# Attention moved 21 turns sooner in a graph layer paced by gathers, with TensorE's last stages written out by hand

## What is computed

```
msg   = relu(x[src] + edge_attr @ w_e + b_e)         # a gathered row of x for each edge
agg   = segment_sum(msg, dst)
local = bn(relu((x + agg) @ w1 + b1) @ w2 + b2 + x)
attn  = bn(attention within graphs of 32 nodes, 4 heads (x) @ out_w.T + out_b + x)
out   = local + attn
out   = bn(out + relu(out @ m_w1 + m_b1) @ m_w2 + m_b2)
y     = layernorm(x + out)
```

## Time and profile before

| | |
|---|---|
| device time, median of 3 runs | 1297.24 us (1296.20 to 1297.25) |
| profiled execution | 1296.03 us |
| its span, first to last instruction | 1294.2 us |
| TensorE busy | 1154.5 us (89%) |
| POOL busy | 944.9 us (73%) |
| VectorE / ScalarE busy | 826.7 us (64%) / 541.2 us (42%) |
| mean granted TensorE clock | 0.969 |

### The profile page before, as it was taken

One profiled execution on the slowest core, in us unless ns is written; L12 is line 12 of the kernel. 1 busy time (PEld: TensorE's weight loads), 2 busy tenths in 40 slices (PEclk: granted clock), 3 DMA queues, 4 the chain that ended last, 5 costly groups with the idle time before them and its releaser, 6 DMA issues.

```text
span 1294.2 us, 28246 instructions
## 1 busy us (share of the span) xinstructions
PE 1154.5 (89%) x7309; PEld 647.4 (50%) x7309; DVE 826.7 (64%) x2090; ACT 541.2 (42%) x1077; POOL 944.9 (73%) x1004
## 2 busy tenths in 40 slices
PE   6787989998899899998989999998989998998896
PEld 3444454544445444444544545454444555765675
DVE  5847486767566576755758666575756667557563
ACT  1343434444344435434344443443434443443353
POOL 7777777777777777777777777777777777675770
PEclk7898999999999999999999999999999998999999
DMA  8554555655555555565555555555655565554550
GB/s 316 154 170 141 175 156 175 174 173 180 170 165 169 164 182 172 160 183 148 183 173 175 165 165 176 166 175 174 172 164 154 183 183 147 168 160 126 175 155 26
DMA packets 119282, 216.50 MB, mean 167 GB/s; under 512 B 24784, under 2 KB 69584, under 8 KB 119120
## 3 DMA queue, kind: packets, MB, share of 16 engines
q0 software_dynamic: 47808, 130.61, 35.0%
q1 hardware_dynamic: 67312, 79.47, 19.6%
q10 hardware_dynamic: 4000, 4.61, 1.0%
HBM read 197.82 MB, written 16.78 MB: 166 GB/s over the span
## 4 chain that ended last, share of the span: by engine, by line
PE 58%; DVE 11%; ACTq 8%; ACT 7%; issue 7%; POOL 6%; DMA 2%; DVEq 0%; SPq 0%
PE bank L837 33%; PE bank L867 12%; PE bank L882 7%; POOL xg L430 6%; ACTq L463 6%; ACT msg L469 4%; DVE bank L681 3%; PE bank L891 3%; ACTq L311 2%; DVE dif L731 2%; DVE mx L726 2%; PE bank L938 1%; DMA xT<-in_xT_dram 1%; DVE aggT L714 1%; ACT kbd L490 1%
## 5 line engine op out<-in xcount | busy, mean ns | idle before, releaser
L430 POOL DMA_INDIRECT xg<-in_x_dram,srcs x996 | 944.0, 948 | 317.4 <-issue 290.0
L469 ACT ACTIVATE msg<-bank 128x512 f32<-128x512 f32 x512 | 277.8, 595 | 543.6 <-PE bank L867 286.7
L681 DVE TENSOR_TENSOR bank<-xg,bank 128x512 f32<-128x512 f32 x498 | 327.4, 690 | 138.1 <-DMA xg<-in_x_dram,srcs 93.0
L867 PE MATMUL bank<-we,ea 64*128 64x256 f32 x2048 | 301.7, 415 | 35.5 <-DVE bank L681 35.5
L867 PEld LDWEIGHTS bank<-we,ea 64*128 64x128 f32 x2048 | 183.1, 192 | 179.7 <-issue 124.1
L714 DVE TENSOR_TENSOR aggT<-bank,aggT 128x64 f32 x512 | 115.2, 225 | 169.1 <-PE bank L891 115.2
L882 PE MATMUL bank<-msg,onehot 128*32 128x256 f32 x2048 | 141.1, 394 | 49.0 <-ACT msg L469 48.4
L837 PE MATMUL bank<-xT,iwT 128*128 128x512 f32 x256 | 128.2, 624 | 7.6 <-DMA xT<-in_xT_dram 4.0
L837 PE MATMUL bank<-o,m 128*128 128x512 f32 (+2 forms) x352 | 125.6, 491 | 4.6 <-DVE o L758 4.4
L882 PEld LDWEIGHTS bank<-msg,onehot 128*32 128x32 f32 x2048 | 54.4, 111 | 141.6 <-ACT msg L469 96.9
L837 PE MATMUL bank<-h,m 128*128 128x512 f32 (+2 forms) x352 | 116.6, 479 | 2.1 <-ACT h L529 2.1
(11 more groups left out here) (92 smaller groups left out, 938.9 us busy)
## 6 DMA issues: line engine op xcount, KB each, us to landing
rows<-in_x_dram SPq DMA_DIRECT2D x2304, 1.0 KB
ea<-in_ea_dram SPq DMA_DIRECT2D x128, 256.0 KB
rows<-in_x_dram ACTq DMA_DIRECT2D x1280, 1.0 KB
xg<-in_x_dram,srcs POOLq DMA_INDIRECT x996
xT<-in_xT_dram SPq DMA_DIRECT2D x32, 256.0 KB, 4.2
aggT<-in_xT_dram SPq DMA_DIRECT2D x32, 256.0 KB, 4.0
oT_dram<-oT SPq DMA_DIRECT2D x32, 256.0 KB
xn<-in_x_dram SPq DMA_DIRECT2D x32, 256.0 KB
```

The lines of the kernel that those rows point to most:

```text
L430: pool.indirect_dma_start(xg[:, slot % NX, n * C:(n + 1) * C], None, t["x"], bass.IndirectOffsetOnAxis(k.srcs[:, at:at + 1], 0)).then_inc( ...
L469: nc.scalar.activation(msg[:, q % NM, :], EA[q % 4][:, :], ACT.Relu).then_inc(s_msg, 1)
L681: nc.vector.tensor_tensor(EA[q % 4][:, :].rearrange("p (a c) -> p a c", a=2), pair.rearrange("p (a c) -> p a c", a=2), KB[:, 0:C].unsqueez ...
L867: ins = nc.tensor.matmul(EA[(2 * d + pair) % 4][:, two * C:(two + 1) * C], ea[rows, n % NEA, at:at + P], k.we[rows, :], start=False, stop= ...
```

## The change

- Attention runs sooner. Slabs 0 to 3 follow one another every 7 turns (`HEADS_EARLY`, base 7J), with both q, both k and both v products in one turn each; later slabs begin 21 turns sooner than before (base 16J - 33 in place of 16J - 12), spread somewhat differently over their 16 turns. The last slab's av is in turn 221.
- For this `xT` has four slabs in place of three and `oT` three in place of two; `msg` has four slots in place of eight, which frees as much memory. SP loads slabs 1 to 3 in turns 1, 7 and 13, and slab J from 4 on in turn 16J - 38 (before: 16J - 19).
- TensorE's turns 254 on are no loop any more but a list of stages; the out_w half of B for blocks 20 and 21 becomes a stage of its own, `A`. The turns of ScalarE's and VectorE's last stages are moved to go with it.

```
-NM = 8
+NM = 4
-NXT, NOT = 3, 2
+NXT, NOT = 4, 3
-HEADS = {"q": (0, 1), "k": (2, 3), "sc": (4, 6), "soft": (5, 7), "v": (8, 9), "av": (11, 13)}
-HEADS_EARLY = {"q": (0, 1), "k": (2, 3), "sc": (4, 5), "soft": (5, 6), "v": (7, 8), "av": (9, 10)}
+HEADS = {"q": (0, 2), "k": (3, 5), "sc": (6, 8), "soft": (7, 9), "v": (10, 11), "av": (13, 14)}
+HEADS_EARLY = {"q": (0, 0), "k": (1, 1), "sc": (2, 3), "soft": (3, 4), "v": (4, 4), "av": (5, 6)}
+EARLY = 4
 def heads_base(J):
-    return max(16 * J - 12, 12 * J)
+    return 7 * J if J < EARLY else 16 * J - 33
...
     19: {"w1": (250,), "B": (251,), "z": (252,), "m1": (252,), "m2": (253,), "T": (254,),
-         "log": (255,), "y": (256,), "xn": (), "out": (257,)},
-    20: {"w1": (254,), "B": (255,), "z": (256,), "m1": (256,), "m2": (257,), "T": (258,),
-         "log": (259,), "y": (260,), "xn": (252,), "out": (261,)},
-    21: {"w1": (256,), "B": (257,), "z": (258,), "m1": (258,), "m2": (259,), "T": (260,),
-         "log": (260,), "y": (261,), "xn": (), "out": (262,)},
+         "log": (256,), "y": (257,), "xn": (), "out": (258,)},
+    20: {"w1": (255,), "B": (256,), "z": (256,), "m1": (257,), "m2": (258,), "T": (260,),
+         "log": (260,), "y": (261,), "xn": (252,), "out": (262,)},
+    21: {"w1": (256,), "B": (257,), "z": (257,), "m1": (258,), "m2": (259,), "T": (260,),
+         "log": (260,), "y": (262,), "xn": (), "out": (263,)},
...
-                if turn in (2, 12):
-                    load_xT(1 if turn == 2 else 2)
-                if turn % 16 == 13 and NXT <= (turn + 19) // 16 < NJ:
-                    load_xT((turn + 19) // 16)
+                if turn in (1, 7, 13):
+                    load_xT((turn + 5) // 6)
+                if turn % 16 == 10 and NXT <= (turn + 38) // 16 < NJ:
+                    load_xT((turn + 38) // 16)
...
+                if stage == "A":
+                    pe.wait_ge(s_oc, 2 * NJ)
+                    if b < LASTB:
+                        pe.wait_ge(s_h1, before(b + 1, "w1"))
+                    for c, of in chunks(b, "B", use):
+                        product(bank(b, "B")[:, of], CC,
+                                lambda a: k.owT[:, a, c * P:(c + 1) * P],
+                                lambda a: k.oT[:, J % NOT, a, of_slab], start=c == 0,
+                                stop=False, skip=True)
...
-            for turn in range(TURNS):
-                if turn < ND:
-                    products(turn)
+            for turn in range(LAST_TURN):
+                products(turn)
...
+            products(ND - 2)
+            transpose_agg(NG - 2)
+            node(19, "T", 0)
+            products(ND - 1)
+            node(20, "w1", 0)
+            sum_group(NG - 1)
+            node(20, "A", 0)
+            transpose_agg(NG - 1)
+            node(20, "B", 0)
+            node(LASTB, "A", 0)
+            node(LASTB, "w1", 0)
+            node(20, "m1", 0)
+            node(LASTB, "B", 0)
+            node(LASTB, "m1", 0)
+            node(20, "m2", 0)
+            node(LASTB, "m2", 0)
+            node(20, "T", 0)
+            node(LASTB, "T", 0)
```

More of the change, by code:

```diff
@@ L75 @@
     19: {"w1": (250,), "B": (251,), "z": (252,), "m1": (252,), "m2": (253,), "T": (254,),
[5 rows of a table removed]
[5 rows of a table added]
 }
+LAST_TURN = 254
 LASTB = 21
@@ L140, in heads_in @@
     for J in range(NJ):
-        plan = HEADS_EARLY if J < 3 else HEADS
+        plan = HEADS_EARLY if J < EARLY else HEADS
         found += [(J, s, n) for s in stages for n, at in enumerate(plan[s])
@@ L401, in stored @@
                 for n in range(NOT):
-                    sp.wait_ge(s_ost[n], 16 * (IT // NOT))
+                    sp.wait_ge(s_ost[n], 32 * len(range(n, NJ, NOT)))
             with sp.If(sp.value_load(k.bad_i[0:1, 0:1], min_val=0, max_val=1) > 0):
@@ L971, in node @@
                 n0, w = BLOCKS[b]
-                at, to = cols(b), bank(b, stage)
+                at, to = cols(b), bank(b, "B" if stage == "A" else stage)
                 J, of_slab = part(b)
@@ L991, in node @@
                     ins.then_inc(s_p1, 1)
+                if stage == "A":
[7 more added lines that the diff above has]
+                                stop=False, skip=True)
                 if stage == "B":
-                    early = b == LASTB
+                    early = b >= 20
                     if use:
@@ L997, in node @@
                         pe.wait_ge(s_oc, (n0 + w + NB - 1) // NB)
[L998 to L1003, removed]
                         pe.wait_ge(s_h1, before(b + 1, "w1"))
```

## The result

The changed kernel takes 1323.11 us (median of four runs, 1322.04 to 1327.36) against 1297.24, a ratio of 1.0202 [1.0173, 1.023]: slower, as forecast, but by 2.0% and not 0.7%, and 6 us beyond the range. Its profiled execution took 1322.04 us, with a span of 1320.3.

The account below looks back on a forecast made before the run. POOL's gathers were taken to bound the kernel: 1250.7 us plus 24.7 early stalls, 1.5 late stalls and a 27.7 tail gave a span of 1304.6, an execution of 1306 us (0.7% loss). The range was 1293 to 1317.

Parts of the forecast that it names:

- What bounds the kernel: Whole run: POOL's gathers at 1.253 us each set the pace; span is 1250.7 us plus POOL's stalls plus tail.
- the price of a slab: Slabs of seven turns: work 28.0, waits 8.7, slow groups 1.7, in all 38.4 us, 3.3 over the gathers.
- the sum: Early slabs 0 to 3: POOL's stalls of 9.1, 3.3, 3.3 and 9.0 add up to 24.7 us.
- The waits, 8.7 a slab: Early slabs: TensorE's in-order waits for copies, scores, softmax and seeds inside a turn, 8.7 us a slab.
- the upper bound: Early stalls at most 33 us, if ScalarE's row fetches delay copies, about 2 us a slab.
- The slow groups, 1.7 a slab: Early slabs: sc and v groups run slower behind TensorE's waits, 1.7 us more a slab.
- a faster clock: Rival, chance 0.11: less idling keeps TensorE at 2.4 GHz, early stalls fall to 15.5, execution 1297.2 us, no change.
- I expect no more: After the early slabs, from turn 28 on: no further early stalls, later slabs having 16 turns as before.
- The late part and the tail: End of the run: late stalls fall from 11.0 to 1.5 us, the tail from 31.1 to 27.7.
- What would have shown it: Signs: POOL waits some 25 us before 200, 9 between 38 and 58; turn 14's products near 100; tail 27 to 28.
- the ring covers the early slabs: Rival, chance 0.14: the ring of gathered pairs keeps early stalls at 0.8 us; execution 1282.5 us, faster.
- Worse than the sum: Rival, chance 0.2: row fetches delay copies (33 us early), late stalls partly stay (5); execution 1318 us.

Follow-up runs that it names:

- early_only: Kernel before with only the four early slabs every 7 turns and the memory they need; 1329.35 us, 1.0243.
- tail_only: Kernel before with only the written-out order of TensorE's last stages and the turns moved with it; 1292.02 us, 0.9966.
- late_rows: Changed kernel with ScalarE's row fetches begun in turn 28 in place of 3, sets every 44 turns in place of 50; 1365.22 us, 1.0523.
- after_r3: Changed kernel with ScalarE fetching three pairs in place of five, a set in 83 turns, the other two gathered by POOL; 1312.02 us, 1.0116.
- filler_r3: Changed kernel with both idle matmuls in TensorE's waits of slabs 0 to 2 and three of ScalarE's five fetched sets; 1310.21 us, 1.0101.
- filler: Changed kernel with matmuls of no use where TensorE waits for copies and scores of slabs 0 to 2; 1322.2 us, 1.02.
- ring11: Kernel before with eleven pairs in the ring in place of seven and four message slots in place of eight; 1293.75 us, 0.9979.

## Why the prediction was right in kind and wrong in size

**What bounds the kernel: right.** The same form, span = 1250.7 + stalls + tail, gives 1250.7 + 44.6 + 25.6 = 1320.9 for the span of 1320.3, and the pitch of 1.253 us held. early_only shows that the loss is early, tail_only and the 0 of late stalls that the rest, but for its 6.0 in the middle, gains.

**The step that failed** is the price of a slab, "A slab costs 28.0 + 8.7 + 1.7 = 38.4 us, 3.3 more than its gathers". Slabs 1 and 2 cost 7.8 and 7.9 more, so 43. TensorE's timeline shows which terms were too small. From the seeds of turn 6 to those of turn 20, two slabs and 14 turns, its time is as follows (waits: idle time ahead of its groups; slower groups: what groups take beyond the durations of the earlier trace rows; work: the rest):

| us of TensorE | the sum | the change | late_rows | after_r3 | filler_r3 |
|---|---|---|---|---|---|
| work at the speeds of the earlier trace rows | 56.0 | 54.5 | 53.5 | 54.0 | 52.9 |
| waits | 17.4 | 19.5 | 15.5 | 15.3 | 11.1 |
| more in slower groups | 3.4 | 6.9 | 8.2 | 9.9 | 0.8 |
| products not in the sum there | 0 | 4.9 | 4.9 | 4.9 | 4.9, and 8.2 of filler |
| in all | 76.8 | 85.7 | 82.1 | 84.1 | 77.8 |

The 28.0 for the work was 0.8 too large. The other two terms were too small, and one was missing; together 8.9 us:

- *The waits, 8.7 a slab*: they were 9.8. Each copy was counted for itself plus handshakes, with nothing queued ahead of it. The 3.51 us of row fetches stood in the rows, but went into the upper bound alone ("about 2 a slab"). Without them (late_rows) the waits are 4.0 less, 2.0 a slab. The bound's size was near, its place wrong: it belonged in the sum. The plain waits, at 15.5, had been priced 1.9 too high, which hid half of it.
- *The slow groups, 1.7 a slab*: they were 3.5. In slab 1 both v stages stand behind waits, 2.61 and 3.78 us against 1.89. Which groups are slow changes from run to run: with fewer fetches (after_r3) the slow groups grew to 9.9, both v of slab 1 at 3.78, and took back most of what the waits had given.
- *Products without a term*: 4.9 in the two slabs. Two sets that fold constants together, once, in turns 11 and 12 (1.05 and 1.84), and a w1 use of block 0 (1.98), which the sum has in slab 3. No run takes these away, so what they cost POOL is not shown.

The v stages and the second fold in the change:

```profile
92.26 2.61 PE L839 MATMUL bank<-iwT,xT 128*128 128x256 f32 x8 [1.79 <-DVE dif L733]
95.54 3.78 PE L839 MATMUL bank<-iwT,xT 128*128 128x256 f32 x8 [0.68 <-ACT qT L503]
...
102.09 1.84 PE L839 MATMUL bank<-c,m 128*128 128x1 f32 x16
```

early_only, with the same early turns, repeats the column of the change within 0.2. The rest of the early miss of 38.5 - 24.7 = 13.8 us lies in slab 0, 2.4, of which 2.2 go with a slow q1 that early_only has not, and in slab 3, 2.3, which is gone without the fetches. The theory that fetches and clock share the miss holds, but how much is whose can't be split, since in slabs 1 and 2 the two runs together give far more than apart.

**The clock.** Groups behind a wait run in part at the lower of the two levels, 1.2 GHz (granted 0.50, 1.94 us against 1.07 for a sum); filler kept the sums and scores of slabs 0 and 2 at 1.07 to 1.09 us and raised the mean of the first 200 us from 0.90 to 0.95. The Trainium skill ("TensorE: Matmul & The Clock Gate", Part 1) says that sustained activity lifts the clock; filler agrees, with the 0.95 beside it. As the rival "a faster clock" used it, that the change itself would idle less, the trace disagrees: the change made more waits, and its clock fell from 0.969 to 0.961.

**"I expect no more" from turn 28 on: wrong by 6.0.** The later slabs still have 16 turns, but stages and blocks fall on each other differently. early_only, with the old placement and all fetches, has 0; after_r3, with the new placement and fewer fetches, has 0. So by these two runs it takes both together. Which stage of the new placement it is was not tried.

**The late part and the tail: right.** Forecast 1.5 and 27.7, measured 0 and 25.6. The order alone gives 3.6 of the tail (tail_only), for the 3.4 of the sum; the copy of the last sums comes 3.9 after the seeds (4.0 forecast), and from there to the last store's source 1318.02 - 1301.15 = 16.9 (18.3). ring11 adds what the prediction had not seen: without the attention moved, taking the late stalls away gains 1.7 us of the 11.

**What would have shown it** was named rightly: waits before 200 us, of which the first in slab 0 (10.6 between 38 and 62, for the 9), none late, a tail of some 27. Turn 14's products came at 109.63, not near 100; 6.9 of that is what the first two slabs lost beyond the sum.

**The rivals.** That the ring covers the early slabs is refuted by the first 60 us. "Worse than the sum" (1318) was nearest: its row fetches are real, its late stalls are not.

The sum, term by term: 38.5 for 24.7, 6.0 for 0 in the middle, 0 for 1.5, 25.6 for 27.7, 0.7 less of gathers: +15.5 of the +15.7 on the span, 1320.3 for 1304.6.

## What to carry to other kernels

Where work is packed into a stretch that the pace already fills, price each wait by everything queued ahead of the one that releases it on its own engine, DMA issues included, price the groups behind the wait at the lower clock, and list every product that falls into the stretch, once-only ones too. A resource that had looked free (ScalarE at 42%) decided how long waits there took. Before a difference between two runs is given to a cause, look for a run that repeats the stretch without it. And before a stall is counted as a loss, give it a longer buffer: if the tail grows by as much, the engine behind it is what is late.

## What was not expected of the hardware

Six row fetches hold ScalarE's queue for 3.57 us, 0.59 each, and everything behind them in order; one pair's fetches fewer shortened the median by 3.8 us in a version whose POOL hardly stalled (2.0 us, then 0). Matmuls of no use put into waits made the useful ones after them faster (1.94 to 1.07 us for a sum), with no cost that shows in the early stalls, but the kernel's time did not fall (1322.2 us). And fewer fetches made TensorE's waits shorter and more of its groups slow: waits 19.5 to 15.3 us, slower groups 6.9 to 9.9.
